# Moving the key and query loads to ScalarE's DMA queue in a gated cross-attention kernel

## The reference, cut to what matters

```python
# x: (16, 128, 1024), ctx_4096: (16, 128, 1024), all float32; 16 heads, 4 parts each
x = x + tanh(g_xattn[0]) * xattn(layernorm(x), ctx_4096, ctx_4096, Wq, ..., Wo, bo)
x = x + tanh(g_ffn[0])  * ffn(layernorm(x), W_org, lora_down, lora_up, lora_keys, Wq2)

def xattn(q, k, v, ...):              # b=16, s=128, H=16, M=4, dk=16
    qh, kh, vh = proj(q), proj(k), proj(v)            # each (b, H, s, dk, M)
    qh, kh, vh = (y + 0.1 * amp * einsum('bhsdi,hij->bhsdj', y, interference) for y in (qh, kh, vh))
    scores = einsum('bhqdm,bhkdm->bhqkm', qh, kh) / sqrt(dk)
    weights = softmax(scores, axis=3)                 # over the keys
    out = einsum('bhqkm,bhkdm->bhqdm', weights, vh)
    return out.reshape(b, s, dm) @ Wo.T + bo

def ffn(x, ...):                      # base matmul plus a mixture of 8 low-rank experts per batch
    base = einsum('bsi,oi->bso', x, W_org)
    coeffs = softmax(einsum('bk,ek->be', mean(x) @ Wq2.T, lora_keys) / sqrt(128))
    return base + einsum('be,bser,ero->bso', coeffs, einsum('bsi,eir->bser', x, lora_down), lora_up)
```

## Time and profile before

| | us |
|---|---|
| three runs | 1502.76, 1509.28, 1512.76 |
| median | 1509.28 |
| the profiled execution's own time | 1509.39 |
| its span (first to last instruction) | 1507.6 |
| TensorE busy | 1406.9 (93%) |
| VectorE, ScalarE, GpSimd busy | 676.9, 397.7, 234.0 |
| mean granted TensorE clock | 0.966 |

### The profile page before, as it was taken

The page is one execution under the profiler, slowest core; times in us unless marked ns, Lnnn a source line. Parts: engine busy times, 40 slices in busy tenths (PEclk is TensorE's granted clock), DMA queues, the critical chain, the costliest instruction groups (busy, mean ns, idle before and its releaser), DMA issues. The chain is left out here.

```text
span 1507.6 us, 22265 instructions
## 1 busy us (share of the span) xinstructions
PE 1406.9 (93%) x8592; PEld 1162.2 (77%) x8592; DVE 676.9 (45%) x1377; ACT 397.7 (26%) x736; POOL 234.0 (16%) x400
## 2 busy tenths in 40 slices
PE   7999999999999999479999999999968999999998
PEld 6887887878888888357777777777756888888887
DVE  5322131222555444356566666666666325333210
ACT  3311101011222223134444454445424011110100
POOL 0000000000000000024455555545610000000000
PEclk9999999999999999669999999999968999999999
DMA  6753645545557778756666766656461211211101
GB/s 201 206 166 126 145 149 133 147 135 146 179 154 182 181 166 244 209 160 185 193 196 193 217 205 195 203 183 187 141 244 43 84 70 57 84 42 70 56 28 56
DMA packets 181719, 224.86 MB, mean 149 GB/s; under 512 B 24048, under 2 KB 122352, under 8 KB 181616
## 3 DMA queue, kind: packets, MB, share of 16 engines
q1 hardware_dynamic: 166160, 189.11, 43.0%
q10 hardware_dynamic: 15456, 34.35, 7.2%
HBM read 136.89 MB, written 85.46 MB: 147 GB/s over the span
## 5 line engine op out<-in xcount | busy, mean ns | idle before, releaser
L1005 DVE TRANSPOSE_TENSOR_REDUCE part<-bank 128x16 f32<-128x512 f32 x256 | 170.4, 699 | 54.7 <-PE bank L864 54.3
L963 ACT ACTIVATE probT<-bank 128x512 f32<-128x512 f32 x256 | 138.7, 596 | 122.4 <-PE bank L884 122.3
L155 PE MATMUL bank<-place_a,w_hi 128*128 128x512 f32 x384 | 152.0, 396 | 7.9 <-DVE place_a L148 7.9
L506 DVE SCALAR_TENSOR_TENSOR stage_lo<-bank,bias_mixed,stage_hi 128x512 fp32r<-128x512 f32 x64 | 48.1, 751 | 230.2 <-ACT stage_hi L508 230.2
L157 PE MATMUL bank<-place_a,w_lo 128*128 128x512 f32 x384 | 150.3, 391 | 0.0
L156 PE MATMUL bank<-place_a,w_hi 128*128 128x512 f32 x384 | 150.0, 391 | 0.0
L508 ACT ACTIVATE stage_hi<-bank,bias_mixed 128x512 fp32r<-128x512 f32 x64 | 44.1, 689 | 261.6 <-PE bank L157 252.4
L845 PE MATMUL bank<-place_a,oT_hi 128*128 128x512 f32 x256 | 109.8, 429 | 0.8 <-POOL oT_lo L1093 0.7
L155 PE MATMUL bank<-place_a,yT_hi 128*128 128x512 f32 x256 | 102.2, 399 | 1.6 <-DVE place_c L148 1.6
L1287 DVE SCALAR_TENSOR_TENSOR raw_d<-bank,gates,raw_d 128x512 f32<-128x512 f32 x32 | 24.0, 750 | 175.2 <-PE bank L157 175.2
L846 PE MATMUL bank<-place_c,oT_hi 128*128 128x512 f32 x256 | 102.3, 400 | 0.0
(11 more groups left out here) (184 smaller groups left out, 2734.7 us busy)
## 6 DMA issues: line engine op xcount, KB each, us to landing
k_rows<-stage_hi SPq DMA_DIRECT2D x128, 128.0 KB, 2.5
v_pad<-v_out SPq DMA_DIRECT2D x32, 512.0 KB, 2.7
v_place<-v_pad ACTq DMA_DIRECT2D x32, 512.0 KB, 4.2
q_rows<-stage_hi SPq DMA_DIRECT2D x124, 128.0 KB, 2.5
early_q<-q_rows SPq DMA_DIRECT2D x128, 100.0 KB
q_in<-q_rows SPq DMA_DIRECT2D x84, 100.0 KB
early_k<-k_rows SPq DMA_DIRECT2D x42, 196.0 KB
k_in<-k_rows SPq DMA_DIRECT2D x42, 196.0 KB
```

What stands on the lines that cost most here:

```text
L155: nc.tensor.matmul(bank_ap, sh, mh, start=(i == 0), stop=False)
L506: lambda bank: nc.vector.scalar_tensor_tensor(out=lo[:], in0=bank[:], scalar=bias, in1=hi[:].bitcast(F32), op0=ALU.add, op1=ALU.subtract),
L963: act.activation(probT[o % NPT][:, i].rearrange("k a p q -> k (a p q)"), two_bank[i][:], ACT.Exp).then_inc(s_exp, 1)
L1005: dve.tensor_reduce(part[o % NS][:, :, 2 * i:2 * i + 2, :].rearrange("k a p b -> k a (p b)"), one_bank[i][:].rearrange("k (a b t) -> k a b ...
```

## The change

Keys and queries are loaded by ScalarE's queue: `load_oct` moves from SP to ACT and stands behind the exponentials of its slot. Its waits are the same. SP takes over the other transfers: `place_max` comes first in each slot, then one piece of 256 KB: a quarter of a batch's values (`load_v` now takes two DMAs for what one did), a half of the residual rows (`load_xb`), or a half of the result (`store_x2`), each with its own slot lag. The second halves of `load_xb` and `store_x2` are some slots later than before. The early loads go with query jobs `c` = 3 to 6 in place of 4 to 7, `zero_second` with `c` = 2 in place of 4. VectorE scales `bo_row` in slot FIRST_V = 7 in place of slot 1.

```diff
-                    if (g, c) == (NG - 1, 4):
+                    if (g, c) == (NG - 1, 2):
 
                         def zero_second(dve):
                             dve.wait_ge(s_rows, 3 * 16)
                             dve.memset(early_q[1][:].bitcast(F32), 0.0).then_inc(s_cleared, 1)
                         job.dve_pre = zero_second
-                    if g == NG - 1 and c >= KC - EARLY:
-
-                        def load_early(sp, o=c - (KC - EARLY)):
+                    if g == NG - 1 and KC - 1 - EARLY <= c < KC - 1:
+
+                        def load_early(sp, o=c - (KC - 1 - EARLY)):
...
             @block.sync
             def _(sp):
-                def load_oct(o):
-                    if o < KQ:
-                        sp.wait_ge(s_zero[o % 2], 1)
-                    else:
-                        sp.wait_ge(s_two, 2 * (o - KQ) + 2)
-                    load_kq(sp, o, k_in[o % KQ], q_in[o % KQ], s_kq[o % KQ])
+                def load_v(h, piece):
+                    b, cols = h // 2, slice((2 * (h % 2) + piece) * HALF, (2 * (h % 2) + piece + 1) * HALF)
+                    if h >= 4:
+                        sp.wait_ge(s_pv, h - 3)
+                    sp.dma_start(v_place[b % 2][:, cols], v_pad[b * P:(b + 1) * P, cols]).then_inc(s_v[b % 2][h % 2], 16)
+
+                def load_xb(b, out):
+                    cols = slice(out * HALF, (out + 1) * HALF)
+                    if b >= 2:
+                        sp.wait_ge(s_x2st[b % 2][out], 16 * (b // 2))
+                    sp.dma_start(xb[b % 2][:, cols], x_t[b * P:(b + 1) * P, cols]).then_inc(s_xb[b % 2][out], 16)
+
+                def store_x2(b, out):
+                    cols = slice(out * HALF, (out + 1) * HALF)
+                    sp.wait_ge(s_x2, 2 * b + out + 1)
+                    sp.dma_start(x_mid[b * P:(b + 1) * P, cols], xb[b % 2][:, cols]).then_inc(s_x2st[b % 2][out], 16)
...
                 for s in range(SLOTS):
                     if 1 <= s <= OCTS:
                         place_max(s - 1)
-                    if s == EARLY - LAG:
+                    if s == 1:
                         projected(sp)
-                    if EARLY <= s + LAG < OCTS:
-                        load_oct(s + LAG)
-                    if s == EARLY - LAG:
+                    if 1 <= s < 9:
+                        load_v((s - 1) // 2, (s - 1) % 2)
+                    for piece, odd, lag in ((0, 0, 2), (0, 1, 2), (1, 0, 5), (1, 1, 4)):
+                        h = half_at(s, lag)
+                        if h is not None and h % 2 == odd and h + 4 < HALVES:
+                            load_v(h + 4, piece)
+                    for out, lag in ((0, O_LAG + 4), (1, O_LAG + 7)):
+                        h = half_at(s, lag)
+                        if h is not None and h % 2:
+                            store_x2(h // 2, out)
+                    for out, lag in ((0, -1), (1, 3)):
+                        h = half_at(s, lag)
+                        if h is not None and h % 2:
+                            load_xb(h // 2, out)
+                    if s == 1:
                         sp.dma_start(bo_row[:], bo.partition_broadcast(P)).then_inc(s_bo, 16)
...
                 def values(h):
                     b = h // 2
                     pe.wait_ge(s_exp, 8 * h + 8)
-                    pe.wait_ge(s_v[b % 2][h % 2], 16 * (b // 2 + 1))
+                    pe.wait_ge(s_v[b % 2][h % 2], 32 * (b // 2 + 1))
...
                     # ACT, behind the two exponentials of the slot
-                    if s < 4:
-                        load_v(s)
-                    h = half_at(s, 0)
-                    if h is not None and h + 4 < HALVES:
-                        load_v(h + 4)
+                    if EARLY <= s + LAG < OCTS:
+                        load_oct(s + LAG)
...
-                    for out, lag in ((0, O_LAG + 4), (1, O_LAG + 6)):
-                        h = half_at(s, lag)
-                        if h is not None and h % 2:
-                            store_x2(h // 2, out)
-                    for out, lag in ((0, -1), (1, 1)):
-                        h = half_at(s, lag)
-                        if h is not None and h % 2:
-                            load_xb(h // 2, out)
...
-                    if s == 1:
+                    if s == FIRST_V:
                         dve.wait_ge(s_bo, 16)
                         dve.tensor_scalar(bo_row[:], bo_row[:], gates[:, 0:1], None, ALU.mult).then_inc(s_bog, 1)
```

More of the change, by code:

```diff
@@ L181, in build, with load_kq @@
         s_kq = [sem(f"s_kq{i}") for i in range(KQ)]
-        def load_kq(sp, o, k_tile, q_tile, landed):
+        def load_kq(eng, o, k_tile, q_tile, landed):
             b, c = o // NOCT, o % NOCT
@@ L187, in load_kq @@
             q_flat = q_rows[b, c].rearrange("a r f -> (a r) f")
-            sp.dma_start(k_tile[:].rearrange("r p t -> r (p t)").bitcast(F32), k_flat[0:ROWS, :]).then_inc(landed, 16)
-            sp.dma_start(q_tile[0:KROWS, 0].rearrange("r p t -> r (p t)").bitcast(F32),
+            eng.dma_start(k_tile[:].rearrange("r p t -> r (p t)").bitcast(F32), k_flat[0:ROWS, :]).then_inc(landed, 16)
+            eng.dma_start(q_tile[0:KROWS, 0].rearrange("r p t -> r (p t)").bitcast(F32),
                          q_flat[0:KROWS, :]).then_inc(landed, 16)
-            sp.dma_start(q_tile[STACK:ROWS, 1].rearrange("r p t -> r (p t)").bitcast(F32),
+            eng.dma_start(q_tile[STACK:ROWS, 1].rearrange("r p t -> r (p t)").bitcast(F32),
                          q_flat[KROWS:2 * KROWS, :]).then_inc(landed, 16)
@@ L927, in gate, with load_oct @@
                     act.activation(gated[:], o_bank[out][:], ACT.Copy, scale=gates[:, 0:1]).then_inc(s_y, 1)
[L929 to L942, removed]
+                def load_oct(o):
+                    if o < KQ:
+                        act.wait_ge(s_zero[o % 2], 1)
+                    else:
+                        act.wait_ge(s_two, 2 * (o - KQ) + 2)
+                    load_kq(act, o, k_in[o % KQ], q_in[o % KQ], s_kq[o % KQ])
                 for store in last_store:
```

## The result

| | before | after |
|---|---|---|
| median of the runs, us | 1506.02 (1502.44 to 1512.76, 4 runs) | 1540.60 (1538.19 to 1552.76, 4 runs) |
| profiled execution: own time, span | 1509.39, 1507.6 | 1538.19, 1536.3 |

The ratio is 1.024, with a 95% interval of 1.017 to 1.031. The change makes the kernel slower; by more or by less than 2% the interval leaves open. 2.7% less had been forecast (1469), with 1454 to 1496 as the range.

A forecast was written before the change was run, and what follows sets the result against it. PE was taken to set the pace, its steady idle time owed to DMA waits. Steady part 25.6, start 11 and ramp 4.5, less 0.75 for bias scaling, made 40.4 us: 1509.4 to 1469.0, range 1454 to 1496.

The forecast's parts named there:

- The steady part: the maximum: Steady attention: the maximum's write lands in 2.5 to 3 us, removing 14.5 of PE's 16.5 us of waits.
- Keys and queries: Steady attention: loads start about 1 us or more sooner from ACT, gaining 6 of 8.8 us of PE waits.
- ScalarE's issue time: Steady attention: load issues take ACT's time; cost between 0 and 11 us, taken as 0.
- The clock: Steady attention: three clock dips follow PE's waits and go with them, gaining 5.1 us.
- The start: Start of attention: the 12.4 us wait goes and octant 4 starts 9.4 us sooner; 11 us gained.
- The ramp: Attention, 646 to 680 us: 3 us of waits and 1.5 us of clock go; 4.5 us gained.
- The terms at nothing: Extra value DMAs, moved halves of `load_xb` and `store_x2`, and their SP waits: issued well ahead, no cost.
- (a): Rival: order in a queue matters little, steady and ramp waits stay, only the start gains; 1499 us, chance 0.11.
- (c): Rival: ACT becomes the bound, load issues held there delay exponentials and the second pass; 1531 us, chance 0.06.

The follow-up runs named there:

- Kernel 2: The change, with values, residual rows and results also on ScalarE's queue, unsplit, leaving SP the maximum and small w_down pieces; 1660.07 us, ratio 1.102.
- kernel 6: The change with key and query loads back on SP, between maximum and piece, ScalarE issuing no steady DMA; 1476.02 us, ratio 0.979.
- kernel 3: The change, with ScalarE's loads of a slot also waiting until that slot's maximum is computed; 1498.12 us, ratio 0.996.
- kernel 4: The kernel before, with a slot's loads put ahead of its maximum on SP from slot 8 on; 1602.35 us, ratio 1.065.
- 7: The change with only the high half (one row) of the maximum written; 1511.20 us, ratio 1.004.
- 8: Kernel 2 with only the high half (one row) of the maximum written; 1610.18 us, ratio 1.069.
- kernel 9: As kernel 6, but from slot 9 on the piece goes ahead of the key and query loads; 1485.51 us, ratio 0.989.

## Why the prediction was wrong

The step that failed is "The steady part: the maximum". It read the 1.3 us between 3.85 and 2.5 us as the work of the 396 KB ahead in the maximum's own queue, and concluded that a shorter queue would bring the write in 2.5 to 3 us. It took 3.95 us in the mean, where it had taken 3.37, and 5.84 us in the slot shown. Kernel 2 shows that a short queue is no shield (8.5 us with no bulk in it), kernel 6 that a long one need not harm, and kernel 3 that the order in time decides: what delays the write is bulk issued shortly ahead of it, on either queue. So +33 us of waits came where -14.5 was summed. The rows could have warned of it: 0.4 us ahead of the write that was read, 512 KB of values were issued on the other queue, and the 2.5 us are those of another transfer in another phase, no base for this one.

"Keys and queries" was right, and for the same reason fatal. It forecast that the loads start some 1 to 2 us sooner and that their waits go; they went from 8.8 to 0 (6 had been taken). That the loads would thereby move ahead of the maximum in time was the very thing that the step described, and the sum never charged the maximum for it. Its other worry, ScalarE's issue time, was worth nothing: 0.3 us of waits, as before.

"The clock": the dips do follow the waits, but there are more waits. In the steady part the clock record of the trace has the lower of the two levels (1.2 GHz) in 11 stretches, 44 us in all, after the change, and in 3, 10 us in all, before; the clock of 0.95 in place of 0.99 says the same. Where 5.1 us of gain were summed, PE's busy time grew by 13 us. Kernel 6 has 2 such stretches, 7 us.

"The start" was forecast at 11 us and measured at 6.1. Octant 4's first pass came at 629.8 and not at 626.5: PE waited 2.9 us for the last query job's result, and the loads behind `projected`, issued from 622.0 and not 620.6, took 7.8 us where 5.5 to 6.5 had been estimated. The mechanism was right, the size not. That the moved early loads push back the stores that both wait for fits the 1.4 us, but no run had the old early loads beside the new bias.

"The ramp" was forecast to gain 4.5 us. Its clock stayed at 0.70 and the first three rounds of four slots, from the first multiplication by the values to the fourth, took 51.9 us in place of 45.4, with waits for the maximum in each. The terms at nothing held: no wait for values, bias or residual rows came up.

Of the rivals, (a) held the right suspicion, that both queues share one path; but it stopped at "no gain" where the same thought, with the loads ahead in time, gives a loss. (c), the one slower case, had the wrong mechanism. The slower case that mattered, "the maximum is overtaken", was argued away by the length of a queue. The rule of turns by packet (the Trainium skill, "DMA: Bandwidth & Descriptors", section "Queues, rings and completion order") was given as what would let a small write in a short queue pass a long one; in kernel 2 it did not pass. Whether turns have a part in the delay stays open (kernels 3, 4, 7 and 8).

## What to carry to other kernels

Before moving a bulk transfer earlier or to another queue, list what small transfer with a deadline it will now be issued ahead of; the queue it stands in does not protect the small one. Here one queue that issues the small and urgent write first, then the loads, then the small pieces beat every split over two queues that was tried: 1476 us against 1486, 1498, 1541 and 1660. Holding back one transfer (kernel 3) or swapping two (kernel 9 against 6) is worth trying before an arrangement of queues is given up. And read more than one slot: here one kind of slot in four carried most of the waits.

## What the runs showed of the hardware

A write of 8 KB that had no bulk in its own queue landed 8.5 us after its issue (mean of 15 writes of kernel 2) with 1560 KB issued in the 3.3 us ahead of it on the other queue, about the time in which those drain at 200 GB/s. The Trainium skill, "DMA: Bandwidth & Descriptors", section "Queues, rings and completion order", says that the write of the completion semaphore lands only behind every earlier write of that DMA engine, across its queues. That would give such a line across queues, and no rule of turns would help against it; the runs fit it, but none separates it from a plain backlog inside the engines, and bytes alone do not set the time: octant 47's write took 4.78 us before with 1420 KB issued in the 3.3 us ahead, and 5.84 after with 1304 KB that were in part newer.

A DMA's issue on ScalarE's queue goes beside its running operation: in the steady part of the change 302 of the 324 issues overlap one, they take 0.36 us in the median (one took 2.1), three a slot, and PE never waited more than 0.4 us for ScalarE.

Before the three dips of the kernel before, PE had waited 1.3 to 1.8 us within some 3 us (once in one wait of 1.8), and around one of them the clock is 0.66 over 5 us. What waits bring with them in slower matmuls can be estimated from PE's busy time for each matmul: 0.106 us before, 0.109 after, 0.115 in kernel 4 and 0.102 in kernel 6. Over 3,400 matmuls that is 12 us for the 24 us more of idle time after the change, and 43 us for the 67 us more of waits of kernel 4 against kernel 6: half to two thirds as much again.
